# Operands of split matrix products placed at one address modulo 256

## The chip, the core and the metric

The kernel runs on one core of a Trainium2 chip. The metric is the device time of one execution in microseconds (us), taken as the median of several runs. The engines are TensorE (PE: matrix products; PEld: its loads of the stationary operand), VectorE (DVE), ScalarE (ACT), GpSimd (POOL) and SyncE (SP, which issues most of the DMAs). SBUF, the on-chip memory, has 128 partitions; an operand's address is its byte offset in a partition, the same for all 128. This text is about the low eight bits of such offsets, called the residue here: the address modulo 256.

## The reference, cut to what matters

```
x = x + routed_by_token(layernorm(x), token_ids, ctx)   # 4 experts, their weights are slices of ctx
x = x + ffn(layernorm(x), w_gv, w_out)                  # quantised: bf16 products are exact
x = x + attention(layernorm(x), ctx, Wq, Wg, Wkv, Wo)   # linear attention, 16 heads, gated
x = x + moe(layernorm(x), gate_w, w_gate, w_up, w_down, shared weights)
# attention: q = x Wq', gate = sigmoid(x Wg' + bg), k, v = ctx Wkv'; out = attn * gate @ Wo'
# moe: softmax, top 4 of 16 experts, 256 slots each; inner width 352; shared expert of width 704
```

x is 4 x 512 tokens of width 512, and all of it is float32. Everything but the second line is computed to nearly float32 accuracy.

## The kernel before

**Split products.** A float32 operand is kept as two tiles of type fp32r (4 bytes an element): a high part `_h`, rounded by ScalarE, and a low part `_l`, the remainder, subtracted by VectorE. A product of two such operands is three matrix products that add up in one PSUM bank, issued by the helper `mm3` (lines 50 to 56): high with high (L54), high with low (L55 or L56), low with high. Each has a stationary operand, which PE loads first (an LDWEIGHTS of up to 128 columns, 512 bytes of each partition), and a moving operand, which it streams (512 columns, 2048 bytes of each partition, or 256 columns in the routed experts). PE loads the next matmul's stationary operand while the current matmul streams. So two reads of SBUF run side by side: the moving operand of matmul n and the stationary one of matmul n+1. In a row of the profile `bank<-a,b` the two names stand in alphabetical order, not in their roles.

**Stages, in order, all on one queue of PE.** With the count of split products of 128 stationary columns and 512 (or 256) moving ones, from the loops:

- front, keys and values of the context: stationary `ctx_h/l_all`, moving `wkv_h/l`; 16 tiles x 2 halves x 4 x 3 = 384 matmuls, in runs of 24 (`project`, L496; `kept_tile`)
- experts of layer 0, on 19 sorted tiles: first product (`expand`, L567), stationary `e0_x_h/l`, moving the context; second product (`contract`, L585), stationary `e0_m_h/l`, moving the context; 19 x 12 = 228 matmuls each, in runs of 12, between transposes of four matmuls (L561, L582)
- the quantised feed-forward, bf16 (L1473, L1494)
- attention, on 16 tiles: queries (stationary `a1_wq`, moving `xT`), output (stationary `a1_aT`, moving `a1_wo`) and gates (stationary `xT`, moving `a1_wg`); 3 x 192 = 576 matmuls, 36 in a row in a turn
- shared expert: gate and up (stationary `s1_wg`, `s1_wu`, `s1_wlast`, moving `xT`), 528 matmuls in long runs; down (stationary `s1_m`, moving `s1_wd`), 272
- 16 routed experts, two of them in turn (u = 0 and u = 1 have buffers of their own): gate and up (stationary `e1_wg`, `e1_wu`, moving `e1_xT`) with 256 moving columns: 768 matmuls with 128 stationary columns and 384 with 96 (`e_expand`); down (stationary `e1_m`, moving `e1_wd`), 270 of 512 columns, 18 in a row, and in the last expert 36 of 256 columns (`contract_last`). The gate weights of one expert are `[P, KD * FF]`: four rows (k = 0 to 3) of 352 columns, 1408 bytes each.

**Placement.** Every tile has a fixed address. `constants` (L59) allocates the first ones one behind the other; the class `Cursor` (L113) hands out the rest from a start rounded up to 64 bytes. The starts are `g.w3_at` (L2812, the region of the bf16 weights, reused for attention, shared and routed weights), `g.ctx_at`, `g.kept_at`, `g.xT_at` and `g.rows_at` (L2815 to L2829), and `raw_q_at` in `ffn0_to_experts1`. The tiles' sizes here are multiples of 256, but for short ones, so a region's start gives the residue of all in it. What comes out of it in the kernel before (the difference is the next stationary address less the moving address, modulo 256):

| products | stationary | moving | difference |
|---|---|---|---|
| context keys and values | 224 | 128 | 96 |
| layer 0 experts, first | 224 | 224 | 0 |
| layer 0 experts, second | 128 | 224 | 160 |
| attention, queries | 192 | 96 | 96 |
| attention, output | 64 | 192 | 128 |
| attention, gates | 96 | 192 | 160 |
| shared expert, gate and up (last chunk) | 192 (128) | 96 | 96 (32) |
| shared expert, down, chunks 0 to 3 (4, 5) | 128 | 192 (128) | 192 (0) |
| routed experts, gate and up, u = 0 | 192 and 64 in turn (k even, odd) | 192 | 0 and 128 |
| routed experts, gate and up, u = 1 | 128 and 0 in turn | 128 | 0 and 128 |
| routed experts, down, u = 0 (high, low part) | 128 | 192, 128 | 192, 0 |
| routed experts, down, u = 1 | 128 | 128 | 0 |

Of the kernel before, what the change touches and what calls it, by code (L numbers as in the profile page):

```python
# [20 lines left out]
AHEAD = 2  # L21

# [9 lines left out]
FT = 3  # L32
FLAST = FF - 2 * P
# [25 lines left out]
def f(ap):  # L59

    return ap.bitcast(fp32)


def constants(nc, g, ctx):
# [20 lines left out]
    g.wscale = sb("wscale", [P, 2], fp32)  # L85

# [42 lines left out]
def front_experts0(nc, g, io):  # L129
# [3 lines left out]
    with ctx:  # L133
# [51 lines left out]
        xn = low.some(2, "e0_xn", [P, D], fp32)  # L185
        x_h, x_l = low.some(2, "e0_x_h", [P, KD, P], f32r), low.some(2, "e0_x_l", [P, KD, P], f32r)
# [666 lines left out]
def ffn0_to_experts1(nc, g, io):  # L853
# [3 lines left out]
    with ctx:  # L857
# [33 lines left out]
        a_var, a_rstd, first_silu = single(1)[0], single(1)[0], single(1)[0]  # L891

        r_raw, r_hl = low.take("a1_r_raw", [P, KD, E1], fp32), low.take("a1_r_hl", [P, KD, 2 * E1], f32r)
        dz, z = low.take("a1_dz", [P, HEADS], fp32), low.take("a1_z", [P, HEADS], fp32)
        a_stats, a_mv = low.take("a1_stats", [P, 6], fp32), low.take("a1_mv", [P, 2], fp32)
# [3 lines left out]
        summ = after_wq.take("a1_summ", [P, KD, 2, SW], f32r)  # L899
        aT = [after_wq.take(f"a1_aT_{n}", [P, KD, P], f32r) for n in "hl"]  # L900
# [101 lines left out]
        with nc.Block() as block:  # L1002
# [688 lines left out]
            def _(v):  # L1691
# [186 lines left out]
                def a_statistics(s):  # L1878
# [5 lines left out]
                    v.bn_aggr(a_mv[:, :], a_stats[:, :]).then_inc(amv_ready, 1)  # L1884
# [156 lines left out]
def shared_experts1(nc, g, io, sem, at):  # L2041
# [48 lines left out]
    for u, where in enumerate((after_routing, after_xT)):  # L2090
        raw_g.append(where.take(f"e1_raw_g{u}", [P, KD * FF], fp32))
        raw_u.append(where.take(f"e1_raw_u{u}", [P, KD * FF], fp32))
        raw_d.append(where.take(f"e1_raw_d{u}", [P, FT, D], fp32))
    xg = [after_routing.some(2, f"e1_xg{t}_", [P, D], fp32) for t in range(2)]
    e_wg, e_wu = [[[where.take(f"e1_{n}_{part}{u}", [P, KD * FF], f32r) for part in "hl"] for u, where in enumerate((after_w, after_xT))]
# [75 lines left out]
    def sync(sp):  # L2171
# [5 lines left out]
        def load(i, u):  # L2177
            e = i * 2 + u
            sp.dma_start(raw_g[u][:, :], io["ew_gate"][bass.ds(e, 1), :, :, :].rearrange("a p k n -> (a p) (k n)")).then_inc(e_raw_in[u], 16)
            sp.dma_start(raw_u[u][:, :], io["ew_up"][bass.ds(e, 1), :, :, :].rearrange("a p k n -> (a p) (k n)")).then_inc(e_raw_in[u], 16)  # L2180
# [92 lines left out]
    def scalar(act):  # L2273
# [22 lines left out]
        def e_split_w(e, part):  # L2296
# [4 lines left out]
            if part < 2:  # L2301
                e_raw, w = ((raw_g, e_wg), (raw_u, e_wu))[part]
                act.activation(w[u][0][:, :], e_raw[u][:, :], ACT.Copy).then_inc(e_w_hi[part][u], 1)
# [62 lines left out]
    def tensor(pe):  # L2366
# [67 lines left out]
        def e_expand(e, c):  # L2434
# [9 lines left out]
            for half, w in enumerate((e_wg[u], e_wu[u])):  # L2444
# [3 lines left out]
                for k in range(KD):  # L2448
                    last = mm3(pe, bank, [x[:, k * FF + c * P:k * FF + c * P + r] for x in w],
# [68 lines left out]
    def vector(v):  # L2518
# [199 lines left out]
        def e_split_w(e, part):  # L2718
# [4 lines left out]
            if part < 2:  # L2723
                e_raw, w = ((raw_g, e_wg), (raw_u, e_wu))[part]
                v.tensor_tensor(w[u][1][:, :], e_raw[u][:, :], f(w[u][0][:, :]), ALU.subtract).then_inc(e_w_lo[part][u], 1)
# [151 lines left out]
```

## Time and profile before

| | |
|---|---|
| median of 3 runs | 1033.46 us (1033.01 to 1033.61) |
| span of the profiled execution, first to last instruction | 1031.0 us |
| PE busy | 1016.8 us, 99% of the span, 5715 matmuls |
| PEld busy | 803.6 us, 78% |
| DVE, ACT, POOL busy | 695.3, 597.7, 282.2 us (67, 58, 27%) |
| granted PE clock | 9 tenths or more of full speed in each of the 40 slices |

The profile gives a span, not a time of its own for the profiled execution; what lies around the span is taken as the median less the span, 1033.46 - 1031.0 = 2.5 us. Matmuls are pipelined: a row of one matmul shows the time from its start to its end, which overlaps the next one's. What a matmul costs in a dense run is the time from its start to the start of the next, called its pitch here. It is read from the first column of the timeline, over many matmuls at a time, since that column is rounded to 0.01 us. The first matmul after a transpose or a short product is shown to start about 0.1 us early, so counts begin with the second.

### The profile page before, as it was taken

What the parts mean: (1) busy time and instruction counts of PE and PEld (TensorE: products, weight loads), DVE (VectorE), ACT (ScalarE), POOL (GpSimd) and SP (SyncE); (2) the same over time, 40 slices, a digit from 0 to 9 for tenths busy, and PEclk for the clock granted to TensorE, in tenths of its full rate; (3) what the DMA queues carried; (4) which work ended last, traced back from release to release, by engine and by line L of the source; (5) the groups of instructions that cost most, each with busy time, mean ns of one, the idle gap of its engine ahead of it and who ended that gap; (6) DMA issues with size and microseconds to landing.
All of it is one profiled execution on the core that took longest, in us unless ns stands there. A gap on an engine that the chain in (4) does not pass through costs nothing.

```text
span 1031.0 us, 16274 instructions
## 1 busy us (share of the span) xinstructions
PE 1016.8 (99%) x5715; PEld 803.6 (78%) x5738; DVE 695.3 (67%) x1371; ACT 597.7 (58%) x953; POOL 282.2 (27%) x444
## 2 busy tenths in 40 slices
PE   9999999999999999999999999999999999999996
PEld 6888888876555555588888888888888999999996
DVE  6757555538999998678777775677724666666662
ACT  6776788746889998863433344111203466666662
POOL 1022222124655553110000034100010154555542
PEclk9999999999999999999999999999999999999999
DMA  6693666522000000301111342302052688888863
GB/s 230 241 336 113 185 184 196 164 72 84 21 26 28 22 21 1 102 13 64 60 63 52 107 129 83 118 11 82 1 194 107 206 233 226 232 247 249 234 156 47
DMA packets 50340, 127.29 MB, mean 123 GB/s; under 512 B 5857, under 2 KB 9953, under 8 KB 49505
## 3 DMA queue, kind: packets, MB, share of 16 engines
q1 hardware_dynamic: 39248, 97.79, 28.4%
q0 software_dynamic: 10448, 27.58, 11.3%
q10 hardware_dynamic: 576, 1.05, 0.3%
q8 instruction: 39, 0.64, 0.3%
q14 instruction: 29, 0.23, 0.1%
HBM read 98.02 MB, written 28.38 MB: 123 GB/s over the span
## 4 chain that ended last, share of the span: by engine, by line
PE 73%; DVE 1%; issue 0%; ACT 0%; POOL 0%; DVEq 0%; ACTq 0%
PE bank L54 17%; PE bank L56 17%; PE bank L55 17%; PE bank L1473 9%; PE bank L1494 5%; PE bank L2431 1%; PE bank L1485 1%; PE bank L1554 1%; PE bank L1572 1%; PE bank L1503 1%; PE bank L1541 0%; PE bank L2418 0%; PE bank L2401 0%; PE bank L2402 0%; PE bank L1597 0%
## 5 line engine op out<-in xcount | busy, mean ns | idle before, releaser
L1473 PE MATMUL bank<-w,f_qT 128*128 128x512 bf16 x496 | 116.0, 379 | 1.4 <-DVE f_h L1769 0.6
L2253 POOL DMA_INDIRECT out<-e_y,scatter_idx x32 | 69.0, 2157 | 110.0 <-ACT e_y L2360 90.0
L1473 PEld LDWEIGHTS bank<-w,f_qT 128*128 128x128 bf16 x512 | 48.5, 98 | 51.2 <-issue 1.0
L2236 POOL DMA_INDIRECT e_xg<-xn_rows,gather_idx x32 | 32.3, 1009 | 166.3 <-DVE gather_idx L2639 99.3
L2291 ACT ACTIVATE s_m_h<-s_mid 128x512 fp32r<-128x512 f32 (+1 forms) x24 | 15.2, 631 | 107.6 <-DVE s_mid L2649 59.9
L2757 DVE TENSOR_TENSOR e_mid<-bank,e_sil 128x256 f32<-128x256 f32 (+1 forms) x47 | 19.7, 420 | 59.9 <-ACT e_sil L2330 51.8
L1494 PE MATMUL bank<-w,f_q2T 128*128 128x512 bf16 x249 | 57.3, 379 | 0.7 <-ACT f_q2T L1199 0.3
L54 PE MATMUL bank<-e_xT_h,e_wg_h 128*128 128x256 f32 (+1 forms) x192 | 55.3, 288 | 0.0
L1769 DVE SCALAR_TENSOR_TENSOR f_h<-bank,f_columns,f_sg 128x512 f32<-128x512 f32 x64 | 47.9, 749 | 10.9 <-PE bank L1473 5.4
L56 PE MATMUL bank<-e_xT_h,e_wg_l 128*128 128x256 f32 (+1 forms) x192 | 54.1, 282 | 0.0
L55 PE MATMUL bank<-e_xT_l,e_wu_h 128*128 128x256 f32 (+1 forms) x192 | 54.1, 282 | 0.0
L55 PE MATMUL bank<-e_xT_l,e_wg_h 128*128 128x256 f32 (+1 forms) x192 | 54.0, 281 | 0.0
L54 PE MATMUL bank<-e_xT_h,e_wu_h 128*128 128x256 f32 (+1 forms) x192 | 53.9, 281 | 0.0
L56 PE MATMUL bank<-e_xT_h,e_wu_l 128*128 128x256 f32 (+1 forms) x192 | 53.9, 281 | 0.0
L54 PE MATMUL bank<-wkv_h,ctx_h_all 128*128 128x512 f32 x120 | 48.4, 404 | 1.7 <-PEq L95 1.4
L1136 POOL TENSOR_TENSOR f_columns<-f_columns,minus_half 128x1 f32<-128x1 f32 x16 | 8.8, 548 | 150.3 <-DVE f_columns L1886 150.3
L1183 ACT ACTIVATE f_sg<-bank,f_columns 128x512 f32<-128x512 f32 x64 | 43.6, 683 | 9.9 <-issue 4.5
L1494 PEld LDWEIGHTS bank<-w,f_q2T 128*128 128x128 bf16 x256 | 24.9, 98 | 30.6 <-issue 0.8
L56 PE MATMUL bank<-wkv_h,ctx_l_all 128*128 128x512 f32 x120 | 47.5, 396 | 0.0
L55 PE MATMUL bank<-wkv_l,ctx_h_all 128*128 128x512 f32 x120 | 47.5, 396 | 0.0
L2330 ACT ACTIVATE e_sil<-bank 128x256 f32<-128x256 f32 (+1 forms) x47 | 18.0, 383 | 45.0 <-PE bank L56 45.0
L2649 DVE TENSOR_TENSOR s_mid<-bank,s_sil 128x512 f32<-128x512 f32 (+1 forms) x24 | 16.6, 691 | 38.0 <-PE bank L56 25.3
(466 smaller groups left out, 3309.8 us busy)
## 6 DMA issues: line engine op xcount, KB each, us to landing
wraw<-in_wffn SPq DMA_DIRECT2D x48, 512.0 KB, 4.2
e_raw_g<-in_ew_gate SPq DMA_DIRECT2D x16, 704.0 KB
e_raw_u<-in_ew_up SPq DMA_DIRECT2D x16, 704.0 KB
e_raw_d<-in_ew_down SPq DMA_DIRECT2D x16, 512.0 KB
sorted_y<-e_y SPq DMA_DIRECT2D x19, 256.0 KB
x_rows<-rows SPq DMA_DIRECT2D x16, 256.0 KB, 2.0
xn_rows<-a_work SPq DMA_DIRECT2D x16, 256.0 KB, 2.0
s_raw<-x_rows SPq DMA_DIRECT2D x16, 256.0 KB, 2.7
```

Source lines behind the costliest of these rows:

```text
L54: pe.matmul(out, ah, bh, start=first, stop=False)
L55: pe.matmul(out, ah, bl, start=False, stop=False)
L56: return pe.matmul(out, al, bh, start=False, stop=last)
L1183: act.activation(sg[c % 2][:, :], gbank[c % 2][:, :], ACT.Silu, scale=deq[t % 3][:, 0:1]).then_inc(sg_ready, 1)
L1473: ins = pe.matmul(bank[c % 2][:, :], qT[t % 2][:, k * P:(k + 1) * P], w_gv(k, col + c * 512), start=(k == 0), stop=(k == KD - 1))
L1494: ins = pe.matmul(obank[:, :], q2T[:, k * P:(k + 1) * P], w_out[:, k, :], start=(k == 0), stop=(k == HID // P - 1))
L1769: v.scalar_tensor_tensor(out=h2[t % 2][:, c * 512:(c + 1) * 512], in0=vbank[c % 2][:, :], scalar=deq[t % 3][:, 0:1], in1=sg[c % 2][:, :], ...
L2236: gp.indirect_dma_start(xg[t][u][:, :], None, g.xn_dram, bass.IndirectOffsetOnAxis(g.gather_idx[:, slot:slot + 1], 0)).then_inc(e_arrived[ ...
L2253: gp.indirect_dma_start(io["out"], bass.IndirectOffsetOnAxis(g.scatter_idx[:, slot:slot + 1], 0), e_y[t][u][:, :], None, compute_op=ALU.ad ...
L2330: act.activation(e_sil[n][0:r, :], hbank[n][0:r, 0:CAP], ACT.Silu).then_inc(e_sil_ready, 1)
L2649: v.tensor_tensor(mid[n % 2][r, :], up[r, :], sil[n % 2][r, :], ALU.mult).then_inc(mid_ready, 1)
L2757: v.tensor_tensor(e_mid[n][0:r, :], hbank[n][0:r, CAP:2 * CAP], e_sil[n][0:r, :], ALU.mult).then_inc(e_mid_ready, 1)
```

## The change

It moves tiles so that every operand of the 512- and 256-column split products starts at residue 128, and so that the routed gate and up weights have rows of 384 columns (1536 bytes = 6 x 256) of which 352 are used.

```
+LINE = 128
+FROW = FT * P
@@ constants
+    g.even = sb("even", [P, 8], fp32)
+def line_up(at):
+    return at + (LINE - at) % (2 * LINE)
@@ class Cursor
+    def line_up(self):
+        self.at = line_up(self.at)
@@ front_experts0
         xn = low.some(2, "e0_xn", [P, D], fp32)
+        low.line_up()
         x_h, x_l = low.some(2, "e0_x_h", [P, KD, P], f32r), low.some(2, "e0_x_l", [P, KD, P], f32r)
@@ ffn0_to_experts1
+        a_stats, a_mv = stats[0], column[:, 62:64]
-        a_stats, a_mv = low.take("a1_stats", [P, 6], fp32), low.take("a1_mv", [P, 2], fp32)
         summ = after_wq.take("a1_summ", [P, KD, 2, SW], f32r)
+        after_wq.line_up()
         aT = [after_wq.take(f"a1_aT_{n}", [P, KD, P], f32r) for n in "hl"]
@@ shared_experts1
-        raw_g.append(where.take(f"e1_raw_g{u}", [P, KD * FF], fp32))
+        raw_g.append(where.take(f"e1_raw_g{u}", [P, KD, FF], fp32))
-    e_wg, e_wu = [[[where.take(f"e1_{n}_{part}{u}", [P, KD * FF], f32r) ...
+    e_wg, e_wu = [[[where.take(f"e1_{n}_{part}{u}", [P, KD, FROW], f32r) ...
@@ e_expand
-                    last = mm3(pe, bank, [x[:, k * FF + c * P:k * FF + c * P + r] for x in w],
+                    last = mm3(pe, bank, [x[:, k, c * P:c * P + r] for x in w],
@@ split of the routed weights, ACT and DVE
-                act.activation(w[u][0][:, :], e_raw[u][:, :], ACT.Copy)
+                act.activation(w[u][0][:, :, 0:FF], e_raw[u][:, :, :], ACT.Copy)
-                v.tensor_tensor(w[u][1][:, :], e_raw[u][:, :], f(w[u][0][:, :]), ALU.subtract)
+                v.tensor_tensor(w[u][1][:, :, 0:FF], e_raw[u][:, :, :], f(w[u][0][:, :, 0:FF]), ALU.subtract)
@@ program
-        g.w3_at = (nc.sbuf_usable_end - 2 * 3 * HID * KD) // 64 * 64
+        g.w3_at = line_up(nc.sbuf_usable_end - 2 * 3 * HID * KD - 2 * LINE + 1)
-            g.ctx_at = (nc.sbuf_base + 63) // 64 * 64
+            before = nc.sbuf_base
+            keep(contexts, "even_ctx", [P, (line_up(before) - before) // 4], fp32)
+            g.ctx_at = line_up(before)
-            g.kept_at = (nc.sbuf_base + 4 * (2 * TT * E1 + 3 * SLOTS) + 2 * 4 * D + 63) // 64 * 64
+            g.kept_at = before + 4 * (2 * TT * E1 + 3 * SLOTS) + 2 * 4 * KD * T + 2 * 4 * D
```

In addresses: the contexts go from 224 to 128; the 32 bytes of `g.even` move `xT` from 96 to 128; the region of `g.w3_at` goes from 192 to 128; taking away `a1_stats` and `a1_mv` (64 bytes) moves the region of `raw_q_at` from 192 to 128; `aT` goes from 64 to 128 and `e0_x` from 224 to 128. `wkv`, `e0_m`, `s1_m`, `e1_m` and the buffers of u = 1 stay at 128. The difference of every pair in the table above becomes 0. No instruction is added or taken away, no wait and no DMA changes, and the order of every queue is the same.

## Rows read from the trace of the kernel before

**Rows 1.** The page, busy time of each engine, share of the span, instructions.
```profile
PE 1016.8 (99%) x5715; PEld 803.6 (78%) x5738; DVE 695.3 (67%) x1371; ACT 597.7 (58%) x953; POOL 282.2 (27%) x444
```
**Rows 2.** PE's longest wait in total: releaser, total us, times, longest us.
```profile
PE bank L54 <- PEq L95: 1.4, 1, 1.4
```
**Rows 3.** Timeline of PE, quantised feed-forward: start us, us, engine, line, operands.
```profile
330.83 1.67 PE L1473 MATMUL bank<-w,f_qT 128*128 128x512 bf16 x7
332.34 0.60 PE L1503 MATMUL bank<-ident,f_xn 128*128 128x128 f32 x4
```
**Rows 4.** Timeline of PE, layer 0 experts, first product, difference 0.
```profile
150.41 0.39 PE L55 MATMUL bank<-ctx_l_all,e_x_h 128*128 x1
...
151.57 0.39 PE L54 MATMUL bank<-ctx_h_all,e_x_h 128*128 x1
...
152.93 0.60 PE L561 MATMUL bank<-ident,e_xn 128*128 128x128 f32 x4
```
**Rows 5.** Timeline of PE, layer 0 experts, second product, difference 160.
```profile
153.60 0.40 PE L55 MATMUL bank<-ctx_l_all,e_m_h 128*128 x1
...
155.94 0.39 PE L56 MATMUL bank<-ctx_h_all,e_m_l 128*128 x1
```
**Rows 6.** Timeline of PE, context keys and values, difference 96.
```profile
69.89 0.39 PE L54 MATMUL bank<-wkv_h,ctx_h_all 128*128 128x512 f32 x1
...
74.58 0.39 PE L56 MATMUL bank<-wkv_h,ctx_l_all 128*128 128x512 f32 x1
```
**Rows 7.** Timeline of PE, one turn of attention: queries, output, gates.
```profile
547.25 0.40 PE L56 MATMUL bank<-xT_h,a_wq_l 128*128 128x512 f32 x1
...
554.95 0.39 PE L56 MATMUL bank<-a_wg_h,xT_l 128*128 128x512 f32 x1
```
**Rows 8.** Timeline of PE, shared expert, gate and up, difference 96.
```profile
669.61 0.40 PE L54 MATMUL bank<-xT_h,s_wu_h 128*128 128x512 f32 x1
...
682.97 0.40 PE L54 MATMUL bank<-xT_h,s_wg_h 128*128 128x512 f32 x1
```
**Rows 9.** Timeline of PE, shared expert, down, one tile (differences 192 and 0).
```profile
700.92 0.40 PE L54 MATMUL bank<-s_wd_h,s_m_h 128*128 128x512 f32 x1
...
704.85 0.39 PE L54 MATMUL bank<-s_wd_h,s_m_h 128*128 128x512 f32 x1
```
**Rows 10.** Timeline of PE, routed down: u = 1 first, then u = 0.
```profile
859.04 0.39 PE L54 MATMUL bank<-e_wd_h,e_m_h 128*128 128x512 f32 x1
...
863.18 0.28 PE L54 MATMUL bank<-e_xT_h,e_wg_h 128*128 128x256 f32 x1
...
872.62 0.40 PE L54 MATMUL bank<-e_wd_h,e_m_h 128*128 128x512 f32 x1
...
876.81 0.28 PE L54 MATMUL bank<-e_xT_h,e_wg_h 128*128 128x256 f32 x1
```
**Rows 11.** Timeline of PE, routed gate and up; then the last expert's down, difference 0.
```profile
866.04 1.03 PE L2431 MATMUL bank<-ident,e_xg 128*128 128x128 f32 x8
...
867.03 0.28 PE L55 MATMUL bank<-e_xT_l,e_wg_h 128*96 128x256 f32 x1
...
869.74 0.28 PE L54 MATMUL bank<-e_xT_h,e_wg_h 128*128 128x256 f32 x1
...
869.98 0.29 PE L56 MATMUL bank<-e_xT_h,e_wg_l 128*128 128x256 f32 x1
870.11 0.28 PE L54 MATMUL bank<-e_xT_h,e_wg_h 128*128 128x256 f32 x1
...
1020.02 0.28 PE L56 MATMUL bank<-e_wd_h,e_m_l 96*128 96x256 f32 x1
...
1022.54 0.28 PE L56 MATMUL bank<-e_wd_h,e_m_l 96*128 96x256 f32 x1
```
**Rows 12.** Busy us (instructions) of each engine by stretch; last: granted clock, DMA share, GB/s.
```profile
500.00:640.00 140.00, 140.00 (x747) 116.51 (x746) 100.95 (x275) 55.81 (x134) 24.97 (x28) 1.00 0.27 87
...
760.00:900.00 140.00, 140.00 (x895) 126.38 (x894) 77.09 (x107) 72.83 (x116) 40.95 (x26) 1.00 0.68 207
```

More of the change, by code:

```diff
@@ L1883, in a_statistics @@
                     v.wait_ge(astats_ready, s + 1)
-                    v.bn_aggr(a_mv[:, :], a_stats[:, :]).then_inc(amv_ready, 1)
+                    v.bn_aggr(a_mv, a_stats[:, :]).then_inc(amv_ready, 1)
                     v.wait_ge(amv_ready, s + 1)
@@ L2090, in shared_experts1 @@
     for u, where in enumerate((after_routing, after_xT)):
-        raw_g.append(where.take(f"e1_raw_g{u}", [P, KD * FF], fp32))
-        raw_u.append(where.take(f"e1_raw_u{u}", [P, KD * FF], fp32))
+        raw_g.append(where.take(f"e1_raw_g{u}", [P, KD, FF], fp32))
+        raw_u.append(where.take(f"e1_raw_u{u}", [P, KD, FF], fp32))
         raw_d.append(where.take(f"e1_raw_d{u}", [P, FT, D], fp32))
     xg = [after_routing.some(2, f"e1_xg{t}_", [P, D], fp32) for t in range(2)]
-    e_wg, e_wu = [[[where.take(f"e1_{n}_{part}{u}", [P, KD * FF], f32r) for part in "hl"] for u, where in enumerate((after_w, after_xT))]
+    e_wg, e_wu = [[[where.take(f"e1_{n}_{part}{u}", [P, KD, FROW], f32r) for part in "hl"] for u, where in enumerate((after_w, after_xT))]
                   for n in ("wg", "wu")]
@@ L2178, in load @@
             e = i * 2 + u
-            sp.dma_start(raw_g[u][:, :], io["ew_gate"][bass.ds(e, 1), :, :, :].rearrange("a p k n -> (a p) (k n)")).then_inc(e_raw_in[u], 16)
-            sp.dma_start(raw_u[u][:, :], io["ew_up"][bass.ds(e, 1), :, :, :].rearrange("a p k n -> (a p) (k n)")).then_inc(e_raw_in[u], 16)
+            sp.dma_start(raw_g[u][:, :, :].rearrange("p k n -> p (k n)"), io["ew_gate"][bass.ds(e, 1), :, :, :].rearrange("a p k n -> (a p) (k n)")).then_inc(e_raw_in[u], 16)
+            sp.dma_start(raw_u[u][:, :, :].rearrange("p k n -> p (k n)"), io["ew_up"][bass.ds(e, 1), :, :, :].rearrange("a p k n -> (a p) (k n)")).then_inc(e_raw_in[u], 16)
             sp.dma_start(raw_d[u][:, 0:2, :], io["ew_down"][bass.ds(e, 1), 0:2 * P, :].rearrange("a (k p) n -> p (a k) n", p=P)).then_inc(e_raw_in[u], 16)
@@ L2302, in e_split_w @@
                 e_raw, w = ((raw_g, e_wg), (raw_u, e_wu))[part]
-                act.activation(w[u][0][:, :], e_raw[u][:, :], ACT.Copy).then_inc(e_w_hi[part][u], 1)
+                act.activation(w[u][0][:, :, 0:FF], e_raw[u][:, :, :], ACT.Copy).then_inc(e_w_hi[part][u], 1)
             else:
@@ L2724, in e_split_w @@
                 e_raw, w = ((raw_g, e_wg), (raw_u, e_wu))[part]
-                v.tensor_tensor(w[u][1][:, :], e_raw[u][:, :], f(w[u][0][:, :]), ALU.subtract).then_inc(e_w_lo[part][u], 1)
+                v.tensor_tensor(w[u][1][:, :, 0:FF], e_raw[u][:, :, :], f(w[u][0][:, :, 0:FF]), ALU.subtract).then_inc(e_w_lo[part][u], 1)
             else:
```

## The prediction

> **What bounds the kernel.** I read the page first: PE is busy in 1016.8 of 1031.0 us, every other engine in 67% or less [rows 1]. Then PE's waits: the longest total for one releaser is 1.4 us, in one wait [rows 2]. So nearly the whole span is PE streaming on one queue, and what an edit takes from PE's pitch it takes from the time. Then the timeline of PE alone, for the pitch in each kind of run. The reader is to see there that the pitch isn't the same for equal shapes.
>
> A bf16 matmul of 512 columns costs 332.34 - 330.83 = 1.51 us for 7, 215.7 ns [rows 3]. The split products of the same shape cost more, and by different amounts. Context keys and values (difference 96): 4.69 us for 20, 234.5 ns [rows 6]. Shared gate and up (96): 13.36 us for 57, 234.4 ns [rows 8]. Attention (96, 128 and 160 in one turn): 7.70 us for 33, 233.3 ns [rows 7]. Layer 0's second product (160): 2.34 us for 10, 234.0 ns [rows 5].
>
> The first product of layer 0 is the comparison. It has the shape and the moving operand of the second, a stationary operand of the same form, and other work beside it that is much the same; what differs is the stationary residue, 224 instead of 128, so that the difference is 0. It starts slowly, 150.41 to 151.57, 1.16 us for 5 = 232 ns, and then settles: 151.57 to 152.93, 1.36 us for 6 = 226.7 ns [rows 4]. The misaligned run shows no such fall: its mean stays 234.0 ns over 10 [rows 5]. A second comparison holds the stage fixed: the routed down product of u = 1 (all 128) takes 4.14 us for 18, 230.0 ns, that of u = 0 (high part 192 against 128) 4.19 us, 232.8 ns [rows 10]. So the trace of before holds the change's effect in it, in two places.
>
> **The change, part by part.** I take an aligned run of n matmuls as n x 227 ns plus about 35 ns at its start. The start is from the first product: its 11 matmuls from the second on take 2.52 us against 11 x 0.227 = 2.50 [rows 4], some 25 ns more; the hidden first one I put at 10 ns. By this a run of 12 costs 229.9 ns each, one of 24 228.5, one of 36 228.0, a long one 227.4. That the settled pitch lasts beyond the 6 matmuls that the rows show is the choice on which the forecast rests; the other end is the whole first product's mean, 229.1 ns [rows 4], rounded up to 230.4 with its first matmul.
>
> - Context keys and values, 384 matmuls, 8 of which wait for ScalarE at the start: 376 x (234.5 - 228.5) = 2.3 us. With 230.4: 1.5.
> - Layer 0, second product: 228 x (234.0 - 229.9) = 0.9 us. With 230.4: 0.8. The first product has nothing to gain: its difference stays 0, at residue 128 instead of 224; the u = 1 experts, at 128, have stretches of the same kind, so I put this at nothing.
> - Attention, 576 in runs of 36: 576 x (233.3 - 228.0) = 3.1 us. With 230.4: 1.7.
> - Shared gate and up with the last chunk, 528: 528 x (234.4 - 227.4) = 3.7 us. With 230.4: 2.1.
> - Shared down: one tile of 17 matmuls takes 3.93 us, 231.2 ns [rows 9]. Difference 192 seems cheaper than 96 and 160, and the last chunk has only 64 rows, so I take half of what is left: 272 x (231.2 - 228.2) = 0.8 us. With 230.4: 0.2.
> - Routed down, the u = 0 half of 270: 135 x (232.8 - 230.0) = 0.4 us [rows 10], either way.
>
> Sum 11.2 us; with 230.4 everywhere 6.7.
>
> **Routed gate and up (the padded rows).** Here the moving operand has 256 columns. With 128 stationary columns 24 matmuls take 866.04 - 863.18 = 2.86 us, 119.2 ns; with 96 columns 23 take 2.71 us, 117.8 ns [rows 10, 11]. Half of them have difference 0 now, half 128. The only row with all of them at 0 is the last expert's down product, of the same moving width: 21 matmuls in 2.52 us, 120.0 ns [rows 11]. So full alignment is no gain here, rather a small loss: 768 x 0.8 = 0.6 us and, with the 96-column ones drawn toward 119 ns, 384 x 1.2 = 0.4 us; 1.0 us together. The bounds: if the 7 ns of the long runs came off here too, 1152 x 7 = 8 us of gain; if all sat at the worst pitch in the rows, 869.98 to 870.11 = 130 ns, 1152 x 11 = 12.7 us of loss. I stay with 120, the one measured run of this kind.
>
> The other edits cost nothing that PE sees. ScalarE and VectorE write the padded rows as four rows of 352 instead of one of 1408, 32 instructions on each that are no wider than before; in 760 to 900 us they are busy for 72.8 and 77.1 of 140 us [rows 12], which hides even a tenth more on each. Were that cover gone, the split of the next weights would come late and PE would wait before a gate product. Taking the attention statistics from a feed-forward buffer adds no wait. DMAs keep their count, size and queue; destinations move by 32 to 64 bytes. The bf16 products are at 215.7 ns already. Eight transposes of 128 columns fill 1.03 us [rows 11], more than eight quarters of a bf16 matmul of 512 columns (0.43 us), so their streaming doesn't bound them; I put them, and the other short products, at nothing.
>
> **The sum.** 11.2 - 1.0 = 10.2 us off the profiled execution: its span goes from 1031.0 to 1020.8 us. With the 2.5 us around the span that is 1023.3 us, against the median of 1033.46.
>
> A rule speaks against all of this. The Trainium skill, TensorE: Matmul & The Clock Gate, Part 2, step 1, says that PE has two independent read ports and that loading the next weights "doesn't steal SBUF read bandwidth from the running matmul"; SBUF — State Buffer, "Who interferes with whom", says that PE never waits on anyone. By these the residue can't matter and the time stays at 1033.5; the trace disagrees, with 226.7 against 234.0 ns for two runs that differ in it [rows 4, 5].
>
> **The rivals.**
>
> *The gain without the lasting settled pitch* (each stretch of a few matmuls restarts the slow start, since the moving operand changes between high and low and from one k to the next over long runs). For it: aligned routed down products, in runs of 18, reach only 230.0 ns [rows 10], though their third k has 96 rows. Against it: the first product also changes operands at each matmul and settles all the same. Price: 6.7 - 1.0 = 5.7 us, 1027.8 us.
>
> *A wait takes its place.* PE gets 3.1 us shorter in attention, where other engines work in chains with it; in 500 to 640 us VectorE is busy for 101.0 of 140 us [rows 12]. For it: attention alternates short products with transposes that wait for VectorE. Against it: PE is busy for all 140 us of that stretch. If attention gave nothing: 11.2 - 3.1 - 1.0 = 7.1 us, 1026.4 us.
>
> *The residue isn't what separates the runs.* Then the comparison of rows 4 and 5 is one of place (transposes before, what ScalarE does beside), and the change doesn't do what it says. For it: difference 192 costs 231.2 ns in the shared stage and 232.8 in the routed one [rows 9, 10], so the difference alone isn't all. Against it: two comparisons, of two stages, have the same sign. Price 0: 1033.5 us.
>
> *Slower: aligned gate and up products collide.* Moving 256 columns takes little longer than a load of 128 stationary columns, so the two reads run side by side for the whole pitch and in the same residues; with every k at difference 0 the alternation that now breaks this up is gone. If the pitch goes to the worst one seen, 130 ns [rows 11], it costs 12.7 us and, with 11.2 us gained elsewhere, ends at 1035.0 us. It decides from 119.2 + 11.2/1.152 = 129 ns on. Against it: the 120.0 ns of the last expert.
>
> **How the numbers follow.** Forecast 0.62; gain without the settled pitch 0.20; a wait 0.06; no effect 0.08; slower 0.04. Least change that a measurement of this kernel can tell: about 0.2%, 2.1 us. The first three are faster, 0.88; no effect is within it, 0.08; slower 0.04. The range reaches below to 1020.5, a part of the 7 ns in the routed products (3 of the 8 us), and above to 1029.0, past the two weaker gains; what it leaves out is no effect and slower, 0.12, and little of the rest.
>
> **What would show it.** In the profile after: the pitch of shared gate and up over some 57 matmuls at 227 to 228 ns (right), 230 to 231 (first rival), 234 (third); context keys and values 228.5 over a run of 24; layer 0's second product no longer different from the first; attention's turn at 228 and its VectorE waits still under 1 us; routed gate and up at 120 ns, where 112 would carry the time below 1018 and 130 above that of before. Counts of instructions and DMAs stay. The forecast is wrong if the long runs aren't below 229 ns, or if PE's waits grow by more than 2 us.

## The result and the profile after

| kernel | median, us | lowest to highest | ratio to before, 95% |
|---|---|---|---|
| before, 4 runs | 1033.47 | 1033.01 to 1033.61 | |
| changed, 4 runs | 1024.04 | 1022.65 to 1025.28 | 0.9910 (0.9899 to 0.9922) |
| changed, repeated as experiment 7, 4 runs (before beside it 1032.92) | 1022.96 | 1022.54 to 1023.81 | 0.9902 (0.9885 to 0.9918) |

The forecast was 1023.3 us, from 1020.5 to 1029.0. The page has the same instructions on every engine and the same bytes of DMA. PE is busy for 1006.3 us, 10.5 us less than before [rows 1]. Its idle time went from 1031.0 - 1016.8 = 14.2 us to 1021.7 - 1006.3 = 15.4 us. The span, 1021.7 us, is 9.3 us shorter.

```profile
PE 1006.3 (98%) x5715; PEld 802.2 (79%) x5738; DVE 694.7 (68%) x1371; ACT 597.0 (58%) x953; POOL 282.3 (28%) x444
```

The timeline of PE after the change, in the places of rows 4 to 11 (start us, us, engine, line, operands). A new helper moved the lines: high with high is L56 here, high with low L57 or L58. Pitches are differences of the first column, divided by the matmuls in between.

```profile
68.00 0.39 PE L57 MATMUL bank<-wkv_l,ctx_h_all 128*128 128x512 f32 x1
...
72.99 0.39 PE L58 MATMUL bank<-wkv_h,ctx_l_all 128*128 128x512 f32 x1
...
149.10 0.40 PE L57 MATMUL bank<-ctx_l_all,e_x_h 128*128 x1
...
151.41 0.39 PE L58 MATMUL bank<-ctx_h_all,e_x_l 128*128 x1
...
152.31 0.39 PE L57 MATMUL bank<-ctx_l_all,e_m_h 128*128 x1
...
154.60 0.40 PE L58 MATMUL bank<-ctx_h_all,e_m_l 128*128 x1
...
543.53 0.40 PE L57 MATMUL bank<-xT_l,a_wq_h 128*128 128x512 f32 x1
...
546.08 0.39 PE L56 MATMUL bank<-a_wo_h,a_aT_h 128*128 128x512 f32 x1
...
551.29 0.39 PE L58 MATMUL bank<-a_wg_h,xT_l 128*128 128x512 f32 x1
...
663.02 0.39 PE L58 MATMUL bank<-xT_h,s_wg_l 128*128 128x512 f32 x1
...
675.94 0.39 PE L58 MATMUL bank<-xT_h,s_wu_l 128*128 128x512 f32 x1
...
694.17 0.39 PE L2415 MATMUL bank<-s_wd_h,s_m_l 128*128 128x512 f32 x1
...
698.02 0.39 PE L2415 MATMUL bank<-s_wd_h,s_m_l 128*128 128x512 f32 x1
...
854.33 0.28 PE L56 MATMUL bank<-e_xT_h,e_wg_h 128*128 128x256 f32 x1
...
857.08 0.28 PE L58 MATMUL bank<-e_xT_h,e_wu_l 128*128 128x256 f32 x1
...
858.19 0.28 PE L57 MATMUL bank<-e_xT_l,e_wg_h 128*96 128x256 f32 x1
...
860.86 0.28 PE L56 MATMUL bank<-e_xT_h,e_wg_h 128*128 128x256 f32 x1
...
863.73 0.40 PE L56 MATMUL bank<-e_wd_h,e_m_h 128*128 128x512 f32 x1
...
867.87 0.28 PE L56 MATMUL bank<-e_xT_h,e_wg_h 128*128 128x256 f32 x1
```

What the reader is to see:

- Shared gate and up: 12.92 us for 57, 226.7 ns, where rows 8 had 234.4. The settled pitch lasts.
- Context: 4.99 us for 22, 226.8 ns, against 234.5 [rows 6].
- Layer 0: the first product 2.31 us for 10, 231.0 ns; the second 2.29 for 10, 229.0 ns, against 234.0 [rows 5]. Both start slowly, and now they are nearly alike.
- Attention: a turn of 34 takes 7.76 us, 228.2 ns, against 233.3 [rows 7]. Its first 11 take 2.55 us, 231.8 ns; the other 23, from 546.08 on, 5.21 us, 226.5 ns. The start costs once per turn.
- Shared down: 3.85 us for 17, 226.5 ns, against 231.2 [rows 9]. Routed down, u = 0: 4.14 us for 18, 230.0 ns, the value of u = 1 before [rows 10].
- Routed gate and up, 128 stationary columns: 2.75 us for 23, 119.6 ns; 96 columns: 2.67 for 23, 116.1 ns, against 119.2 and 117.8 [rows 10, 11].

Summed over whole stages, in both traces. The starts of the weight loads serve as clock marks here, since there is one for each matmul; a matmul counts from the start of the load behind its own to the start of the next load, so waits inside a stage are in its sum.

| products | before, us | after, us | gain | forecast |
|---|---|---|---|---|
| context keys and values, 384 | 92.2 | 90.0 | 2.2 | 2.3 |
| layer 0, first | 52.5 | 52.5 | 0.0 | 0 |
| layer 0, second | 53.2 | 52.3 | 0.9 | 0.9 |
| attention, 576 | 134.4 | 131.7 | 2.7 | 3.1 |
| shared gate, up, last chunk, 528 | 123.6 | 120.2 | 3.4 | 3.7 |
| shared down | 63.0 | 62.1 | 0.9 | 0.8 |
| routed down, 512 columns | 62.5 | 62.2 | 0.3 | 0.4 |
| routed gate and up, 128 stationary columns, 768 | 91.6 | 91.7 | -0.1 | -0.6 |
| the same, 96 columns, 384 | 45.3 | 44.7 | 0.6 | -0.4 |
| sum | | | 10.9 | 10.2 |

10.9 us of product time gone and a span 9.3 us shorter: the rest, some 1.5 us, came back as waits. Of them 1.0 us lies in the summary products of the context stage (k and v of each tile, L534 to L540: 13.8 us before, 14.8 after, summed in the same way). Another 0.4 us lies behind the first product of the quantised feed-forward, where a summary product waits for VectorE (L1461 <- c_k_l); the repeat of the changed kernel, experiment 7, does not have it.

**The new wait.** PE's list of waits after the change (releaser, total us, times, longest):

```profile
PE bank L56 <- PEq L98: 1.5, 1, 1.5
...
PE bank L534 <- DVE v_hl L817: 0.9, 1, 0.9
```

Before, the same wait had 0.3 us. How it came about is seen on ScalarE about 15 us earlier. First the kernel before (ACT, then DVE, then PE; in brackets the idle time before an instruction and its releaser):

```profile
72.92 0.63 ACT L421 ACTIVATE kexp<-kexp 128x512 f32<-128x512 f32 x1 [0.67 <-DVE kexp L792]
```
```profile
73.59 0.69 DVE L798 SCALAR_TENSOR_TENSOR kf<-bank,kexp 128x512 f32<-128x512 f32 x1 [0.70 <-ACT kexp L421]
```
```profile
90.20 0.36 PE L522 MATMUL bank<-v_hl,k_h 128*128 128x258 f32 x1 [0.29 <-DVE v_hl L805]
```

And the changed kernel:

```profile
72.17 1.06 ACT L385 ACTIVATE wraw<-wraw 128x1024 f32<-128x1024 f32 x1 [1.32 <-DMA wraw<-in_wffn]
...
73.23 0.62 ACT L433 ACTIVATE kexp<-kexp 128x512 f32<-128x512 f32 x1
```
```profile
73.88 0.69 DVE L810 SCALAR_TENSOR_TENSOR kf<-bank,kexp 128x512 f32<-128x512 f32 x1 [2.49 <-ACT kexp L433]
```
```profile
89.30 0.36 PE L534 MATMUL bank<-v_hl,k_h 128*128 128x258 f32 x1 [0.89 <-DVE v_hl L817]
```

Through this stage ScalarE also sums the feed-forward weights, in 24 chunks (`measure`, L385), each waiting for its load. These sums stand in order with the exponentials of the key tiles. In the kernel before, the chunk was there when ScalarE came to it: its last sum in this place starts at 71.12 us without a wait. With PE faster, ScalarE comes earlier and waits 1.32 us for the load; the exponential stands behind it, VectorE waits 2.49 us for that, and the chain ends 0.9 us earlier than before where PE's products end 1.5 us earlier (86.83 against 88.33).

### The profile page after: what moved, and what is told of

The parts are those of the page before. It is cut to its first block, busy times and chain, and to the rows that moved or that the text cites. A ratio compares the mean times of both kernels' runs of the same rounds, so it can differ in the third digit from the quotient of the medians.

```text
span 1021.7 us, 16274 instructions
## 1 busy us (share of the span) xinstructions
PE 1006.3 (98%) x5715; PEld 802.2 (79%) x5738; DVE 694.7 (68%) x1371; ACT 597.0 (58%) x953; POOL 282.3 (28%) x444
## 4 chain that ended last, share of the span: by engine, by line
PE 72%; DVE 1%; issue 0%; ACT 0%; POOL 0%; DVEq 0%; ACTq 0%
PE bank L56 17%; PE bank L57 17%; PE bank L58 17%; PE bank L1486 9%; PE bank L1507 5%; PE bank L2444 1%; PE bank L1498 1%; PE bank L1567 1%; PE bank L1585 1%; PE bank L1516 1%; PE bank L1554 0%; PE bank L2431 0%; PE bank L2414 0%; PE bank L2415 0%; PE bank L1610 0%
## 5 line engine op out<-in xcount | busy, mean ns | idle before, releaser
L1486 PE MATMUL bank<-w,f_qT 128*128 128x512 bf16 x496 | 116.0, 379 | 1.5 <-DVE f_h L1782 0.6
L1782 DVE SCALAR_TENSOR_TENSOR f_h<-bank,f_columns,f_sg 128x512 f32<-128x512 f32 x64 | 47.9, 749 | 10.9 <-PE bank L1486 5.3
L56 PE MATMUL bank<-e_xT_h,e_wg_h 128*128 128x256 f32 (+1 forms) x192 | 55.1, 287 | 0.0
L57 PE MATMUL bank<-e_xT_l,e_wu_h 128*128 128x256 f32 (+1 forms) x192 | 54.1, 282 | 0.0
L58 PE MATMUL bank<-e_xT_h,e_wu_l 128*128 128x256 f32 (+1 forms) x192 | 54.0, 281 | 0.0
L56 PE MATMUL bank<-e_xT_h,e_wu_h 128*128 128x256 f32 (+1 forms) x192 | 53.9, 281 | 0.0
L57 PE MATMUL bank<-e_xT_l,e_wg_h 128*128 128x256 f32 (+1 forms) x192 | 53.9, 281 | 0.0
L58 PE MATMUL bank<-e_xT_h,e_wg_l 128*128 128x256 f32 (+1 forms) x192 | 53.9, 281 | 0.0
L56 PE MATMUL bank<-wkv_h,ctx_h_all 128*128 128x512 f32 x120 | 47.7, 398 | 1.8 <-PEq L98 1.5
L57 PE MATMUL bank<-wkv_l,ctx_h_all 128*128 128x512 f32 x120 | 46.8, 390 | 0.0
L58 PE MATMUL bank<-wkv_h,ctx_l_all 128*128 128x512 f32 x120 | 46.8, 390 | 0.0
L2343 ACT ACTIVATE e_sil<-bank 128x256 f32<-128x256 f32 (+1 forms) x47 | 18.0, 382 | 45.3 <-PE bank L58 45.3
```

What stands on the lines that cost most here:

```text
L56: pe.matmul(out, ah, bh, start=first, stop=False)
L57: pe.matmul(out, ah, bl, start=False, stop=False)
L58: return pe.matmul(out, al, bh, start=False, stop=last)
L1486: ins = pe.matmul(bank[c % 2][:, :], qT[t % 2][:, k * P:(k + 1) * P], w_gv(k, col + c * 512), start=(k == 0), stop=(k == KD - 1))
L1782: v.scalar_tensor_tensor(out=h2[t % 2][:, c * 512:(c + 1) * 512], in0=vbank[c % 2][:, :], scalar=deq[t % 3][:, 0:1], in1=sg[c % 2][:, :], ...
L2343: act.activation(e_sil[n][0:r, :], hbank[n][0:r, 0:CAP], ACT.Silu).then_inc(e_sil_ready, 1)
```

## The experiments

Each kernel ran beside the kernel before. The first four shared one chip, where the kernel before had a median of 1033.07 us, the next four a second (1032.92), the last three a third (1033.01). The two maps of the pitch were executed once each.

### 1. The pitch alone, by difference and width

```
for cols, w, r, d in RUNS:      # moving columns, stationary columns, moving residue, difference
    for n in range(24):
        pe.matmul(bank[0][0:w, 0:cols], sta[:, at:at + w], mov[:, r // 4:r // 4 + cols], ...)
    for n in range(4):          # a mark between runs, bf16
        pe.matmul(bank[1][:, 0:128], mark_s, mark_m, ...)
```

> This kernel does none of the reference's work: it writes zeros and runs 32 kinds of runs of 24 equal fp32r matmuls (one stationary, one moving operand, set to 1.0), each run followed by 4 short bf16 matmuls. In order: moving 512 columns at residue 128, stationary 128 columns at a difference of 0, 16, ... 240; moving at residue 0 with differences 0, 96, 128, 192; difference 256; moving 256 columns with differences 0, 32, ... 224; stationary operands of 96, 64 and 32 columns at difference 0 with 512 moving. Theory (the difference modulo 256 alone sets the pitch): difference 0 settles at 226 to 227 ns with the moving operand at 128, at 0, and at difference 256; 96 is 234 at both residues; 160 is 233 and 192 is 229; 256 columns at difference 0 settle at 120. Rival (the absolute residue 128 counts): with the moving operand at 0, difference 0 gives no 227 but 230 or more. Rival (place in the program, other engines' work): all differences cost the same here, since no other engine works. For the rest above 215.7 ns the theory that it comes from the load that runs beside the stream expects it to fall with the stationary columns: 11 ns at 128, some 8 at 96, 5 at 64, 3 at 32; if it is a fixed cost of fp32r it stays 11.

The timeline of PE, one row for each run of 24 and for the mark behind it: difference 0, 16, 96 and 240 at 512 columns, then 0 and 64 at 256 columns.

```profile
6.08 5.71 PE L65 MATMUL bank<-mov,sta 128*128 128x512 f32 x24
11.63 0.40 PE L67 MATMUL bank<-mark_m,mark_s 128*128 128x128 bf16 x4
11.84 5.84 PE L65 MATMUL bank<-mov,sta 128*128 128x512 f32 x24
17.52 0.40 PE L67 MATMUL bank<-mark_m,mark_s 128*128 128x128 bf16 x4
...
41.24 5.86 PE L65 MATMUL bank<-mov,sta 128*128 128x512 f32 x24
46.95 0.40 PE L67 MATMUL bank<-mark_m,mark_s 128*128 128x128 bf16 x4
...
94.08 5.70 PE L65 MATMUL bank<-mov,sta 128*128 128x512 f32 x24
99.61 0.40 PE L67 MATMUL bank<-mark_m,mark_s 128*128 128x128 bf16 x4
...
128.96 3.12 PE L65 MATMUL bank<-mov,sta 128*128 128x256 f32 x24
131.91 0.40 PE L67 MATMUL bank<-mark_m,mark_s 128*128 128x128 bf16 x4
...
135.25 3.01 PE L65 MATMUL bank<-mov,sta 128*128 128x256 f32 x24
138.10 0.40 PE L67 MATMUL bank<-mark_m,mark_s 128*128 128x128 bf16 x4
```

From start to mark, difference 0 takes 5.55 us, 16 takes 5.68, 96 takes 5.71, 240 takes 5.53. At 256 columns difference 0 takes 2.95 us and 64 takes 2.85. The settled pitch, from the starts of the last 12 weight loads of each run, in ns (this run and the finer one, experiment 5):

| difference | 512 x 128 | 256 x 128 | 256 x 96 |
|---|---|---|---|
| 0 | 226.7 | 120.0 | 116.0 |
| 4, 8, 12 | 232.6, 230.5, 230.0 | | |
| 16, 32, 48 | 233.3 each | 118.0, 118.6, 117.8 | 32: 116.7 |
| 64 | 233.3 | 113.3 and 117.8 | 116.7 |
| 80, 96, 112 | 232.1, 234.6, 233.3 | 118.9, 119.0, 120.2 | 96: 120.0 |
| 128, 144, 160 | 232.6, 233.3, 233.3 | 118.5, 120.0, 120.0 | 119.8, -, 117.8 |
| 176, 192, 208 | 230.0, 228.9, 232.0 | 117.9, 117.8, 116.7 | 192: 113.3 |
| 224, 228, 232, 236 | 233.3, 231.1, 231.1, 231.7 | 224: 116.7 | 224: 116.7 |
| 240 | 226.6 and 228.3 | 120.0 | |
| 244, 248, 252 | 233.3 each | | |

What follows: with identical operands in every matmul and nothing beside them, difference 0 is 226.7 ns and nearly all others are 230 to 235. So the pitch depends on the difference of two SBUF addresses modulo 256; the no-effect rival falls. Moving both operands together changed it by 0.7 ns at most: moving at 0 instead of 128 gave 226.7, 234.2, 233.3 and 228.9 for differences 0, 96, 128 and 192, and difference 256 gave 226.7. Fewer stationary columns did not help at difference 0: 230.0 ns with 96 and 64, 231.7 with 32. That refutes the expectation that what lies above bf16's 215.7 ns [rows 3] shrinks with the load.

### 2. x back at residue 96

```
-    g.even = sb("even", [P, 8], fp32)
-            before = nc.sbuf_base
+            before = (nc.sbuf_base + 31) // 32 * 32
```

> The changed kernel with one part undone: the transposed activations xT are back at residue 96, all else at 128. Differences become 32 (queries, shared gate and up, last chunk) and 224 (gates). Theory (difference sets the pitch): 720 matmuls at difference 32 go from 227.4 ns to 231 to 233, 192 at difference 224 to about 230, and the runs that follow in attention and the shared stage start slowly again: 720 x 4.5 ns = 3.2 us, 192 x 2.5 = 0.5 us, restarts 0.5 us; 4.2 us slower than the changed kernel, near 1028.3 us. The front and layer 0 stay at 227 ns. Rival (the weights' residue alone counts, where they lie at 128): no loss, 1024. Rival (only the pair of 96 and 192, 96 apart, is bad): at most 1 us of loss.

1028.23 us (1026.97 to 1030.10), ratio 0.9949 (0.9932 to 0.9965), where theory had 1028.3. The timeline, shared gate and up, with difference 32:

```profile
665.33 0.40 PE L57 MATMUL bank<-xT_l,s_wg_h 128*128 128x512 f32 x1
...
675.13 0.40 PE L57 MATMUL bank<-xT_l,s_wu_h 128*128 128x512 f32 x1
```

Shared gate and up are at 9.80 us for 42, 233.3 ns, as the map has it for 32; the context stage keeps its aligned pitch. 32 bytes of one tile's place carry 4 to 5 us of the gain. One term was off: the gates, at difference 224, were put at 230 ns and went to 233 to 234.

### 3. The routed rows at 352 again

```
-FROW = FT * P
+FROW = FF
```

> The changed kernel with one part undone: the routed gate and up weights have rows of 352 columns again, so that k = 1 and 3 start at residue 0 against a moving operand at 128 (difference 128). Theory (for 256 moving columns alignment is worth nothing or less): within 0.7 us of the changed kernel, 1023.4 to 1024.7 us, and the pitch of 119 ns (128 columns) and 118 (96) in place of a settled 120 and 117. Rival (the padding carries a share of the gain): 1 us or more slower, 1025 us or above.

1022.84 us (1022.17 to 1024.40), ratio 0.9904 (0.9887 to 0.9920): 0.6 us below the range of the theory, which took 1024.04 for the changed kernel; that kernel did not run beside it here. Gate and up took 91.3 us with 128 stationary columns and 45.3 with 96, where the changed kernel has 91.7 and 44.7. The repeat beside the changed kernel (experiment 8) gave 1023.19 (1022.82 to 1023.50), ratio 0.9906 (0.9890 to 0.9923), against 1022.96: the padding is worth nothing that can be measured.

### 4. The context alone

The changes ahead of the quantised feed-forward alone, all later regions where they were.

```
-        low.line_up()
+        low.at += (128 - low.at) % 256
-        g.w3_at = line_up(nc.sbuf_usable_end - 2 * 3 * HID * KD - 2 * LINE + 1)
+        g.w3_at = (nc.sbuf_usable_end - 2 * 3 * HID * KD) // 64 * 64
-            g.ctx_at = line_up(before)
+            g.ctx_at = nc.sbuf_base
```

> The kernel before with one part of the change alone: the contexts and layer 0's transposed rows at residue 128, everything from the feed-forward on as before. Theory: context keys and values at 227 ns from 234.4, 376 matmuls, 2.3 us; layer 0's second product 0.9 us; together 3.2 us faster than before, 1030.2 us, and the later stages unchanged in pitch. Rival (a gain early is given back at the wait between the stages, since the first stage's last stores and weights end it): less than 1 us faster.

1030.72 us (1029.99 to 1031.93), ratio 0.9967 (0.9945 to 0.9989): 2.4 us faster where theory had 3.2 and the rival less than 1. In its trace the context products are down by 2.0 us and layer 0's second by 0.9; the gaps at the summary products are up by 1.4, so that its profiled execution kept less than half of the gain (its span is 1029.8 us).

### 5. The map in steps of 4

The kernel of experiment 1 with other differences.

```
+WIDE = [(512, 128, 128, d) for d in (224, 228, 232, 236, 240, 244, 248, 252, 4, 8, 12)]
+HALF = [(256, 128, 128, d) for d in (16, 40, 48, 56, 60, 64, 68, 72, 80, 112, 144, 176, 208, 240)]
```

> A second map like the first (no work of the reference, zeros written): moving 512 columns at 128 with differences 224 to 252 and 4 to 12 in steps of 4; moving 256 columns at 128 with 128 stationary columns and differences 16, 40, 48, 56, 60, 64, 68, 72, 80, 112, 144, 176, 208, 240, then moving at 64 and at 0 with difference 64; then 96 stationary columns with differences 0, 32, ... 224. The first map gave 226.7 ns at differences 0 and 240 and 233 at 16 and 224; for 256 columns 113.3 at 64 alone, against 120 at 0. Theory (two periodic reads lock in windows of the difference): the window at 0 reaches over 240 to 252 and ends within 4 to 12; the window at 64 for 256 columns is some 16 wide and holds wherever the moving operand lies (113 at 64 and 0 too); 96 columns have a window of their own near 64. Rival (single lucky points): the neighbours of 64 are at 117 to 120, and the moving residues 64 and 0 differ.

The timeline of PE: difference 240 and 252 at 512 columns, then 64 at 256 columns.

```profile
29.59 5.74 PE L64 MATMUL bank<-mov,sta 128*128 128x512 f32 x24
35.17 0.40 PE L66 MATMUL bank<-mark_m,mark_s 128*128 128x128 bf16 x4
...
47.17 5.85 PE L64 MATMUL bank<-mov,sta 128*128 128x512 f32 x24
52.85 0.40 PE L66 MATMUL bank<-mark_m,mark_s 128*128 128x128 bf16 x4
...
86.24 3.07 PE L64 MATMUL bank<-mov,sta 128*128 128x256 f32 x24
89.16 0.40 PE L66 MATMUL bank<-mark_m,mark_s 128*128 128x128 bf16 x4
```

252 takes 5.68 us, as far above 5.55 as 16 does: 0 is a single point, not the middle of a window, and that part of the theory falls. At 256 columns the neighbours of 64 are at 117.8 ns (56), 119.5 (60) and 118.3 (68 and 72), and 64 itself gave 117.8 with the moving operand at 128 and at 64, 113.3 with it at 0. 96 stationary columns have their low pitch at 192, not near 64. 240 takes 5.58 us here and 5.53 in the first map, 64 at 256 columns 2.92 and 2.85. The same operands settle into one of two steady patterns. What decides between them is not shown: the two maps differ in the runs ahead, and they ran on two chips. Experiment 6 bears on it.

### 6. Routed gate and up at difference 64

```
+    after_w.at -= 3 * 64
+    after_xT.at += 64
     e_wg, e_wu = [[[where.take(...)
+    after_w.at += 3 * 64
+    after_xT.at += 3 * 64
```

> The changed kernel with the routed gate and up weights at residue 192 against a moving operand at 128: difference 64 for all k (rows stay 384 wide), all else as in the changed kernel. Theory (the map's pitch holds in the kernel): 768 matmuls with 128 stationary columns go from 119.4 to 113.3 ns, 4.7 us, and the 384 with 96 columns gain or lose 1 us: 1024.0 - 4.7 = 1019.3 us, between 1018.3 and 1020.3. Rival (in the kernel the high, low and 96-column loads in turn break the lock): 1023 to 1024 us. Rival (the stage is bound by weights or VectorE once PE is shorter): PE waits appear, 1021 to 1023 us.

1020.29 us (1019.97 to 1022.13), ratio 0.9876 (0.9860 to 0.9893). The repeat of the changed kernel on the same chip (experiment 7) gave 1022.96 (1022.54 to 1023.81); the ranges don't meet, though the two ratios' intervals overlap. Gate and up with 128 columns fell from 91.7 to 89.1 us, with 96 columns they rose from 44.7 to 45.1. The timeline, two runs of the same products:

```profile
848.36 0.28 PE L56 MATMUL bank<-e_xT_h,e_wg_h 128*128 128x256 f32 x1
...
850.63 0.28 PE L58 MATMUL bank<-e_xT_h,e_wu_l 128*128 128x256 f32 x1
...
855.12 0.28 PE L58 MATMUL bank<-e_xT_h,e_wg_l 128*128 128x256 f32 x1
...
857.60 0.28 PE L58 MATMUL bank<-e_xT_h,e_wu_l 128*128 128x256 f32 x1
```

The first has 2.27 us for 20, 113.5 ns, the second 2.48 for 21, 118.1 ns: only half of the runs find the short pattern. Which half is regular in this trace. The 15 runs that stand behind products of 96 columns settle at 113.3 to 115.0 ns, the 15 behind a down product at 117.8, all with the same residues. So what stands ahead of a run goes with the pattern that it takes; no run changed that alone.

The routed products gave 2.2 us and the median 2.7 us, where theory had 4.7. The time lies within the expected range only because the changed kernel took 1022.96 us beside it and not the 1024.0 that was assumed. It is the fastest kernel of the study.

### 7 and 8. Repeats

> The changed kernel once more, beside the two others: 1023 to 1025 us by every theory.

> The changed kernel with routed rows of 352 columns once more, beside the changed kernel on the same chip. Theory (the padding is worth nothing, for alignment at 256 columns gives no lower pitch): within 0.7 us of it. Rival (the padding costs): more than 0.7 us faster without it. Rival (the padding helps): more than 0.7 us slower.

1022.96 us and 1023.19 us, told above: without the padding 0.2 us slower, as theory had it. In the repeat's trace ScalarE waits for the same chunk until 73.07 us (1.32 us again), VectorE's chain ends when it ended in the kernel before, and the gaps at the summary products are up by 1.3 us.

### 9 and 10. Fewer chunks to sum

The first is the changed kernel, the second the kernel before.

```
+        MEAS = 18
-            return list(range(CHUNKS * (n - 1) // 9, CHUNKS * n // 9)) if 1 <= n <= 9 else []
+            return list(range(MEAS * (n - 1) // 9, MEAS * n // 9)) if 1 <= n <= 9 else []
```

> The changed kernel, with 18 instead of 24 chunks of the feed-forward weights loaded and summed during the context stage (the sums of the last six are left out, so the quantised values differ). Theory A: the context stage gives back part of its 2.2 us because ScalarE's in-order queue holds sums that wait for loads (at 72.17 us after a wait of 1.32 us), the exponential of the next key tile stands behind them, and VectorE and then PE come late. With six loads and sums fewer the loads are never late: the gaps of PE at the summary products (waits on k and v, 1.46 us in the profile of the changed kernel, 1.73 in the repeat, 0.68 before) fall to 0.7 us or less, and the median to 1021.8 to 1022.3 against 1022.96. Rival B: PE is simply faster than VectorE's own chain of some 4.3 us per tile; the gaps stay at 1.4 to 1.7 us and the median at 1022.9.

> The kernel before with the same 18 chunks. Theory A: there PE was late enough for the loads, so little is gained: gaps at the summary products from 0.68 to 0.3 to 0.7 us, median 1032.3 to 1032.9, and the changed kernel's gain over it with 18 chunks is 10.5 us or more, against 10.0 with 24. Rival B: gaps unchanged at 0.7, 1032.9, and the gain stays 10.0.

1024.09 us (1022.48 to 1024.37), ratio to before 0.9910 (0.9894 to 0.9925), and 1034.61 us (1033.33 to 1035.44), ratio 1.0012 (1.0003 to 1.0021). The changed kernel with 18 chunks, ScalarE and PE:

```profile
71.87 0.63 ACT L434 ACTIVATE kexp<-kexp 128x512 f32<-128x512 f32 x1 [1.63 <-DVE kexp L805]
```
```profile
88.78 0.36 PE L535 MATMUL bank<-v_hl,k_h 128*128 128x258 f32 x1 [0.33 <-DVE v_hl L818]
```

The exponential runs 1.36 us earlier and PE's wait is 0.33 us, not 0.89; in the kernel before with 18 chunks it is 0.24, not 0.29. Summed over the stage, the summary products take 13.8 us with 18 chunks and 14.8 with 24 in the changed kernel, and 13.7 and 13.8 in the kernel before: all of the new 1.0 us is gone. The experiment takes away sums as well as loads, but the sum that waited would have cost the exponential next to nothing without its wait: 73.23 - 1.32 = 71.91 us, an estimate, against 71.87. So the late load was the cause of that wait.

The medians do not fall as expected, and most of that is PE's clock. In both profiles PE's granted clock is at half, 1.2 instead of 2.4 GHz, for 3.4 us shortly after the wait at the end of the first program block (L98), here in the changed kernel with 18 chunks:

```profile
222.70:226.10 3.40, 3.40 (x10) 0.50 0.67 192
```

The columns are the stretch, its length, PE's busy time (instructions), the granted clock, the DMA share and GB/s. The matmuls in it come every 427 ns and not every 227, which costs 1.6 us: from 222.56 to 226.20 nine take 3.64 us where 9 x 0.2267 is 2.04. PE had stood idle for 1.87 us before the fall (1.79 in the kernel before with 18 chunks). With 24 chunks the same wait is 1.52 and 1.44 us, and the clock stays at full speed there. What lengthened the wait is open.

The times bear the reading out. Of the changed kernel with 18 chunks, three took 1024.07 to 1024.37 us at a mean granted clock of 0.996 and one 1022.48 at 0.998. Of the kernel before with 18 chunks, six took 1034.61 to 1035.44 at 0.995 to 0.997 and five 1033.33 to 1033.74 at 0.997 to 0.999. The difference of the medians, 10.5 us, is what theory A asked for, against 9.4 and 10.0 with 24 chunks; with spreads of 2 us that supports it but does not prove the size.

### 11. The exponential ahead of the sums

```
                     act.activation(kexp[n % 2][:, :], kexp[n % 2][:, :], ACT.Exp).then_inc(s["kexp_ready"], 1)
+                    if n <= 9:
+                        for c in measured(n - 1):
+                            measure(c)
...
-                    for c in measured(n):
-                        measure(c)
+                    if n == 9:
+                        for c in measured(n):
+                            measure(c)
```

> The changed kernel, all 24 chunks, but on ScalarE's queue the exponential of tile n stands ahead of the sums that belong to tile n-1 (tiles 2 to 9), so that no key tile waits behind a load. Theory A: the gaps at the summary products fall from 1.46 to 1.73 us to 0.7 to 1.0, median 1022.2 to 1022.6. Rival C: the loads are issued only when a sum has freed a buffer, so later sums make later loads and the chain ends as late as before or later; gaps 1.5 us or more, median 1022.9 to 1024.

1036.53 us (1035.62 to 1037.73), ratio 1.0033 (1.0021 to 1.0045): worse by 13 us than the changed kernel. PE's waits in its profile:

```profile
PE bank L538 <- DVE summ L736: 4.6, 1, 4.6
PE bank L566 <- DVE wtot L757: 3.3, 1, 3.3
```

The sums themselves, all 24 of which the total needs, came late, and the splits of v and k behind them too. About 8 us of the loss are these two waits. The rest is mostly the clock: it is at half for 6.8 us twice, from the last 0.2 us of the first wait on and from the last 1.5 us of the second. By an estimate from PE's busy time in these stretches, 6.50 and 5.25 us, that costs 5.9 us. The mean granted clock is 0.991 to 0.994 in the six executions, against 0.997 to 0.998 in those of the changed kernel.

```profile
51.30:58.00 6.70, 6.50 (x20) 0.50 0.49 157
```

Rival C has the direction, but the price is far above its 1024 us. The old order of ScalarE is a tight fit: moving one group by one step costs nearly ten times the wait that it was to mend.

## Why the prediction was right

**That the residue separates the runs**: right. The comparison of rows 4 and 5 was of two places in one trace, and its rival had a chance of 0.08; experiments 1 and 2 settle it. In the map only PE works, and 16 bytes of address move its pitch from 226.7 to 233.3 ns. By the Trainium skill (TensorE: Matmul & The Clock Gate, Part 2, step 1) the load takes no read bandwidth from the stream. The prediction took from it that the residue can't matter, and with that the map doesn't agree. The other rule quoted there, that PE waits on no other engine, says nothing on two reads of PE itself, and the map doesn't test it. What in the reads collides is not shown by any run.

**That the settled pitch lasts** (the choice on which the forecast rested): right, 226.7 ns over 57 matmuls. The rival of 1027.8 us falls. The start, put at 35 ns per run, measured some 20 to 55: attention's first 11 matmuls take 2.55 - 11 x 0.2267 = 0.06 us more than the settled pitch gives and the following 23 nothing more, layer 0's two products 0.04 and 0.02 us. The terms for attention and shared gate and up came out 0.4 and 0.3 us below the forecast; their stage means are 228.6 and 227.7 ns where it had 228.0 and 227.4, and 233.3 and 234.1 before, where it had 233.3 and 234.4.

**Shared down**: 0.9 for 0.8. Half of what was left was taken off for difference 192; the map has it at 228.9, between 0 and the rest, so the row was rightly read.

**Routed gate and up**: the loss of 1.0 us was wrong, it is a gain of 0.5. For 128 columns the step "768 x 0.8" rested on one row at 120.0 ns; the up products do settle there, but the gate products ahead of them mostly do not (118.3 and 119.2 ns in nearly every expert, whichever its buffers), and the stage lost 0.1. For 96 columns the step "drawn toward 119 ns" has the wrong sign: 117.8 became 116.1 ns. The 120.0 ns row was of 128 stationary columns, and the load's width moves the pitch. The collision at 130 ns did not come. Its premise, that 256 moving columns take little longer than a load, can't be read off the rows: in the map a load of 128 columns has a row of 188 ns, and the pitch is 120.

**The other edits at nothing**: right for the padding (experiments 3 and 8).

**A wait takes its place**: forecast for attention, where it did not come. It came in the context stage, whose waits the sum put at nothing, and PE's list of waits was indeed short there [rows 2]. That list shows what PE waited for at its old speed. It does not show that ScalarE's next load was due just behind. About 1.5 us went back as waits, 1.0 of it in this way, within the bound of 2 us that was set. Against the sum of 10.2 us, the routed products gave 1.5 us more, the waits took 1.5 us, and the other products fell short by 0.8. That the first two cancel is luck: without it the sum would have missed by more than the 0.8 us that it did, 10.9 - 1.5 = 9.4 us.

**The 2.5 us around the span**: in each execution whose profile is here, from the changed kernel on, the time is 1.7 us more than the span. The other 0.8 us, by an estimate from these, is how much faster the profiled execution of before was than its median. Since the forecast takes the difference to the median, this leaves it as it was.

**Open**: the mechanism in the reads; why what stands ahead of a run goes with its pattern; and what makes the 1 us between this kernel's two medians (1024.04, 1022.96). No run tells these apart.

## What to carry to other kernels

Where one engine is busy 99% of the time and the same shape shows two pitches in one trace, look for what differs between the places, and try it on the smallest kernel that has nothing else in it; one such map answered here what several whole kernels could only suggest. Align for the shape at hand: difference 0 modulo 256 was best for 512 columns and among the worst for 256, where 64 gained 2.7 us. And before booking a gain on the busy engine, ask what the others will reach sooner: a wait on a load in an in-order queue can be hidden just by the slowness that is being removed. When a variant is slower than its waits explain, read the granted clock by stretch: here 3.4 us at half clock hid the gain of experiment 9.

## What was not expected of the hardware

- One and the same pair of operands has two steady pitches: 113.3 and 117.8 ns (256 columns, difference 64), 226.6 and 228.3 ns (512 columns, difference 240). In experiment 6 both of the first pair stand in one trace, by what ran ahead.
- The clock fell to half for 3.4 us after PE had been idle for 1.8 to 1.9 us, and not after 1.4 to 1.5 us in the same place (experiments 9 and 10, against the kernels with 24 chunks). No run varied the wait alone.
- Narrower stationary operands make a 512-column matmul dearer at difference 0: 226.7 ns with 128 columns, 230.0 with 96 and 64, 231.7 with 32.
- 4 bytes off the best difference cost nearly as much as 96: 232.6 ns at 4, 233.3 at 252, 234.6 at 96.
- With 96 stationary columns and 256 moving ones the best of eight differences is 192 (113.3 ns), and that of the 128-column ones 64, so one placement cannot serve both passes of the routed experts.
